# Three message-passing layers of a graph network: the order of TensorE's steps in the GATv2 loops, and of ScalarE's copies in the GAT loop

## The reference

```python
def _gatv2(x, src, dst, eattr, Wl, Wr, We, att, b, n):
    xl = x @ Wl
    xr = x @ Wr
    xj = xl[src]
    h = leaky_relu(xj + xr[dst] + eattr @ We, 0.2)
    logits = h @ att
    m = segment_max(logits, dst, n)
    ex = exp(logits - m[dst])
    denom = segment_sum(ex, dst, n)
    return segment_sum(xj * (ex / denom[dst])[:, None], dst, n) + b

# GAT, 4 heads of 64
h = (x @ W).reshape(-1, 4, 64)
e = leaky_relu(einsum('nhd,hd->nh', h, att_src)[src] + einsum('nhd,hd->nh', h, att_dst)[dst], 0.2)
m = segment_max(e, dst, n)
ex = exp(e - m[dst])
alpha = ex / segment_sum(ex, dst, n)[dst]
out = sigmoid(segment_sum(alpha[:, :, None] * h[src], dst, n) + bias)
```

## Time and profile before

| | |
|---|---|
| median of 3 runs | 6522.72 us (6521.69 to 6536.36) |
| the profiled execution's own time | 6535.35 us |
| its span in the profile | 6533.6 us |
| mean granted PE clock | 0.941 of full speed |
| busy share | PE 76%, DVE 71%, ACT 51%, POOL 48% |
| the three edge loops | 1474 + 1479 + 1518 = 4471 us |

### The profile page before, as it was taken

How to read it: one execution, slowest core, us unless ns; L and a number is a source line. 1 busy time by engine, 2 the same in 40 slices (tenths; PEclk the granted TensorE clock), 3 DMA queues, 4 the chain that set the end, 5 groups by cost and what they waited for, 6 DMA issues and landing times. The chain is left out here.

```text
span 6533.6 us, 112163 instructions
## 1 busy us (share of the span) xinstructions
PE 4991.3 (76%) x28188; PEld 3639.1 (56%) x28558; DVE 4608.6 (71%) x17132; ACT 3312.4 (51%) x8567; POOL 3155.9 (48%) x3442
## 2 busy tenths in 40 slices
PE   5999877985778777886687877777366766666799
PEld 2444444863656555664465655556255555555578
DVE  8999876254777777776577767777577777777721
ACT  5888765023555555553455545555355555555520
POOL 2444333634556555650565656554255555555400
PEclk9999988997999999998899999999689999999899
DMA  2233334853444444441444444443234443443264
GB/s 57 62 89 100 94 100 143 318 191 95 106 107 109 108 107 106 107 100 36 102 108 108 108 102 108 105 106 80 59 92 103 102 103 101 104 102 103 74 160 114
DMA packets 606739, 698.65 MB, mean 107 GB/s; under 512 B 243043, under 2 KB 512656, under 8 KB 599802
## 3 DMA queue, kind: packets, MB, share of 16 engines
q0 software_dynamic: 128832, 362.75, 22.0%
q1 hardware_dynamic: 477370, 329.75, 18.4%
HBM read 589.91 MB, written 102.19 MB: 106 GB/s over the span
## 5 line engine op out<-in xcount | busy, mean ns | idle before, releaser
L980 POOL DMA_INDIRECT gath<-table,src_col x880 | 846.7, 962 | 873.5 <-issue 601.8
L980 POOL DMA_INDIRECT h<-table,src_col x880 | 841.3, 956 | 574.9 <-issue 574.9
L1119 PE MATMUL psum<-xr 128*128 x3520 | 1031.8, 395 | 35.5 <-ACT xr L1081 18.0
L703 DVE SCALAR_TENSOR_TENSOR xr<-xr,gath,psum 128x259 f32<-128x259 f32 x1440 | 685.8, 476 | 108.0 <-PE psum L687 82.2
L1068 ACT CAST rows<-psum 128x128 bf16<-128x128 f32 x440 | 116.7, 265 | 1134.0 <-remote 684.8
L1204 POOL DMA_INDIRECT gath<-table,src_col x440 | 423.6, 963 | 490.3 <-issue 327.3
L1119 PEld LDWEIGHTS psum<-xr 128*128 128x128 f32 x3520 | 545.8, 196 | 200.5 <-issue 50.2
L999 DVE SCALAR_TENSOR_TENSOR zs<-zs,mean 128x256 f32<-128x256 f32 x1760 | 649.3, 423 | 0.0
L1005 DVE TENSOR_REDUCE seen<-psum 128x1 f32<-128x512 f32 x440 | 303.4, 690 | 470.5 <-PE psum L1130 321.4
L1204 POOL DMA_INDIRECT h<-table,src_col x440 | 422.0, 959 | 297.8 <-issue 297.8
L687 PE MATMUL psum<-zs,locrow 128*128 128x259 f32 x1440 | 468.1, 452 | 117.0 <-POOL zs L642 94.3
(11 more groups left out here) (330 smaller groups left out, 11988.3 us busy)
## 6 DMA issues: line engine op xcount, KB each, us to landing
locrow<-g_locb SPq DMA_DIRECT2D x660, 128.0 KB
pairs<-xr SPq DMA_DIRECT2D x640, 115.5 KB
xr<-pairs SPq DMA_DIRECT2D x13, 1716.0 KB
gath<-table,src_col POOLq DMA_INDIRECT x1320
h<-table,src_col POOLq DMA_INDIRECT x1320
xr<-pairs SPq DMA_DIRECT2D x25, 832.0 KB
acc<-pairs SPq DMA_DIRECT2D x12, 1716.0 KB
xr<-pairs SPq DMA_DIRECT2D x13, 1584.0 KB
```

Source lines behind the costliest of these rows:

```text
L703: nc.vector.scalar_tensor_tensor(kept[:, u, 0:EXTRA + 3], kept[:, (u - 1) % HELD, 0:EXTRA + 3], t["same"][:, g:g + 1], m.ps[u % 4][:, 0:EX ...
L980: pool.indirect_dma_start(m.gath[r][:, j, :], None, table, bass.IndirectOffsetOnAxis(m.src_col[r][:, j:j + 1], 0)).then_inc(gathered[r], 16)
L1119: nc.tensor.matmul(zb[q][:, j, :], m.hot[r][:, j, :], blk(m.xr, b, 0, D), start=True, stop=False)
```

## The change

In both GATv2 loops PE's list gives `turn_parts` a lag of 2 and a place ahead of `sum_group`; before, it stood at the head of the next step with lag 3. In the GAT loop the one-hots' copies go to three buffers in turn, the third a piece of `zs_all` that this loop doesn't use otherwise; `choose` waits for the group sum of three groups ago, `sum_group` reads the same buffer, and `choose` stands ahead of `copy_turned` on ACT.

```diff
--- before.py
+++ after.py
@@ -1140,7 +1140,7 @@
                                           start=(j == 0), stop=(j == T - 1))
                 mm.then_inc(group_sum, 1)
 
-            straight([(3, turn_parts), (4, flip), (3, show_logits), (1, mix), (4, sum_group)],
+            straight([(4, flip), (3, show_logits), (1, mix), (2, turn_parts), (4, sum_group)],
                       blocks_on(nc, m, mybir.EngineType.PE))
 
 
@@ -1170,6 +1170,7 @@
         here_ps = [m.ps[4 + q][:, K:2 * K] for q in (0, 1)]
         sum_ps = [m.ps[4 + q][:, 2 * K:2 * K + WA] for q in (0, 1)]
         rows = m.rows[:, :]
+        chosen_rows = [m.prob[:, 0, :], m.prob[:, 1, :], m.zs_all[:, 0:WIN]]
         room = m.xr3[:, :, :].rearrange("p b c -> p (b c)")
         ohT = [room[:, r * WIN:(r + 1) * WIN] for r in range(RG)]
         lgs = [room[:, RG * WIN + 2 * r * C:RG * WIN + 2 * (r + 1) * C].bitcast(F32) for r in range(RG)]
@@ -1368,15 +1369,15 @@
             def choose(t, u, turn, b):
 
                 act.wait_ge(flipped, t + 1)
-                after(act, group_sum, t, 2)
-                nc.scalar.copy(m.prob[:, u % 2, :], flip_ps[:, :]).then_inc(chosen, 1)
+                after(act, group_sum, t, 3)
+                nc.scalar.copy(chosen_rows[t % 3], flip_ps[:, :]).then_inc(chosen, 1)
 
             def shrinkage(t, u, turn, b):
                 r = u % R
                 act.wait_ge(dropped, t + 1)
                 nc.scalar.activation(m.less[r][:, 0:H], m.drop[:, 0:H], ACT.Exp).then_inc(shrink, 1)
 
-            straight([(4, copy_turned), (7, choose), (8, weigh), (6, shrinkage), (1, mask), (7, exponentials)])
+            straight([(7, choose), (4, copy_turned), (8, weigh), (6, shrinkage), (1, mask), (7, exponentials)])
 
         @block.tensor
         def _(pe):
@@ -1429,7 +1430,7 @@
                 pe.wait_ge(act_weighed, t + 1)
                 after(pe, done, t, 2)
                 for j in range(T):
-                    mm = nc.tensor.matmul(sum_ps[u % 2], m.prob[:, u % 2, j * P:(j + 1) * P], m.gath[u % RG][:, j, 0:WA],
+                    mm = nc.tensor.matmul(sum_ps[u % 2], chosen_rows[t % 3][:, j * P:(j + 1) * P], m.gath[u % RG][:, j, 0:WA],
                                           start=(j == 0), stop=(j == T - 1))
                 mm.then_inc(group_sum, 1)
```

## The result

The changed kernel took **6642.42 us** (median of 4 runs, 6617.16 to 6653.06) against 6522.2 us for the kernel before (6504.22 to 6536.36), a ratio of **1.0181** (95% interval 1.0152 to 1.0209). The profiled execution took 6617.16 us with a span of 6615.4 us, so it is the fastest of the four; the mean granted PE clock was 0.923, against 0.941.

The account below looks back on a forecast made before the run. It took POOL's trains of four gathers and the held release of PE's messages, 6.51 us a step, as the bound; 0 in GATv2 and -4.6 us in GAT gave 6518 us from the median 6522.72, range 6395 to 6625.

Parts of the forecast that it names:

- What bounds the kernel: Gather loops: PE's messages held during trains of four gathers, a period of 6.51 us set by POOL and the release.
- most steps must be like the one at 3256: GATv2 loops: most steps have a held message, as 6.45 and 6.54 us lie near the locked 6.51 us.
- Rival A: GATv2: messages late because of the order, not gathers; show_logits' 436 us of waits go, 6087 us; chance 0.08.
- The wait of show_logits: PE in GATv2 waits 263.1 and 172.8 us for ACT's copy of the turned parts; the change aims there.
- The price in GATv2: Group sum behind the turn waits for DVE's parts; sum and flips end 0.2 to 0.3 us later, 0.8 us to spare.
- Gain in a step in which the message is held: 0: GATv2: the earlier turn gains nothing, as the release hangs on the gathers and ACT's copy starts when it did.
- The term of 0 in the sum: The GATv2 loops' share of the forecast, 2 x 220 groups: no change in time, 0 us.
- The step without held messages: GATv2's new order with no message held: a chain of 5.10 us a step, under 6.51, so it does not bind.
- Rival C: GATv2: the turn's wait becomes the step, 6.96 us for 6.50 in half the steps, 6624 us; chance 0.17.
- in the locked step it comes in 0.03 us: GATv2: show's message reaches DVE in 0.03 us in a locked step, the reason for a chance of no more than 0.17.
- The gain of 4.6 us: GAT loop's end: seven steps without gathers each lose the flips' 0.65 us wait for choose; steps with gathers gain 0.

Follow-up runs that it names:

- e9: Kernel before with the GATv2 loops' gathers left out after the first ten groups, old order: 5920.3 us against 6548.61 us for the kernel before.
- e8: Kernel before with the GATv2 loops' loads of lin, locrow and eaT left out after the first five groups: 6512.92 us against 6548.61 us.
- e2: Kernel before with only the GAT part of the change: 5511.05 us against 5516.34 us, ratio 0.9991.
- e17: Kernel before with only the GAT part of the change, five rounds at the higher level: 6548.98 us against 6540.15 us, ratio 1.0006.
- e18: Kernel before with POOL's GATv2 gathers also waiting for DVE's parts of seven groups before: 6972.49 us against 6527.27 us, ratio 1.0685.
- e5: The whole change once more, against the kernel before at the lower level: 5559.02 us against 5520.4 us, ratio 1.0076.

## Why the prediction was wrong

*What bounds the kernel: right.* PE's messages are late in a train of gathers, and the gathers are the cause: 628 us by e9, against 36 for the loads in e8. One reading went too far: "most steps must be like the one at 3256". The turn ended there 4.24 us into a train of four, and so, within 4.2 to 4.4, it did in 199 of 440 steps; the mean of 6.50 us came from shorter and longer steps too.

The Trainium skill's rule that a DMA never contends with a compute engine ("SBUF — State Buffer", Who interferes with whom) doesn't tell what comes here. The trace agrees with it as to the engines' own work: the copy of the turned parts takes 0.27 us in a held step and in one that isn't. But the end messages of PE come late while gathers run at this level. Rival A, beside which it was named, gave 6087 us and did not come.

*The wait of show_logits: right as to where, wrong as to what follows.* It went (436 to 46 us), and what is late next was `parts`, as said.

*The price in GATv2, "0.2 to 0.3 us later ... with 0.8 us to spare", "Gain in a step in which the message is held: 0": this is the step that failed.* It took one step of the old rhythm, with the next release fixed at 3258.6 and with the messages of mix and show at once, as given, and moved PE's turn inside it. But the rhythm is a product of the order. The old one has the mix end 2.45 us into a train and come at once; the new one has sum, flips and show in a row behind a turn that waits, in many steps no pause that lets POOL's trains end after four, and trains of seven and eight, in one of which the mix is held for 3.9 us. The term of 0 in the sum was +103 us. The turn's wait was put at 0.1 us a step and was 474.6 us over 440 steps, 1.08 us; before, PE had waited 436 us, 0.99 us, in the other place. And the sum took PE's work as fixed, the group sum at 1.73 us: PE was busy for 146 us more, 119 of them in the group sum, while its waits fell by 43 us in all. How much of this is the clock behind the new pauses, and how much the longer trains, no run tells apart.

*The step without held messages, 5.10 us "under 6.51. So the new order alone does not bind": right in size, and of no use as a bound.* At the level of 5516 us it is 5.15 us against 5.06, and there it binds: 52 us. The estimate stood against 4.99 us for the old order in the rows without gathers, a difference of 0.11 us that could have been charged to every step in which nothing is held: 440 x 0.11 = 48 us.

*Rival C came, its number in part by luck.* 6624 us with a chance of 0.17, against 6642 measured. Its mechanism is there: `seen` out of "remote" for 374.2 us, where it was 134.6, and PE idle ahead of L1104. But it was to decide where the show's message is late in most steps, and `seen` came out of "remote" 104 times in 440; PE's longer busy time, 146 us, is not in it. It was held down by "in the locked step it comes in 0.03 us", again the old rhythm taken as fixed. The range ended at 6625 because C was priced for half of the steps; in all of them it would have been 6725, and 0.08 of it was left out.

*GAT: right in the total, not shown in the loop.* PE's wait at the flips (L1422, 383.3 us) is all but gone, and the waits of this loop are now

```profile
ACT ex L1350 <- issue: 452.2, 182, 3.9
...
PE psum L1401 <- DVE seen L1282: 194.7, 151, 2.2
```

so show_first, which waits for DVE's maximum, is late next, as said. The gain of 4.6 us agrees with -5.3 us (e2, interval -10.5 to +0.6 us) and isn't told apart from none. At the higher level the profiles have the loop shorter by some 20 us, more than the 4.6, and e17 as a whole no faster.

## What to carry to other kernels

A wait that is taken out of one place of a cycle through several engines turns up at the next instruction that waits for the same chain; so price a reorder by the chain from the new wait round to itself, at both rhythms that the trace shows, and not inside one old step. Then look at the engine's busy time as well as its waits: here the waits fell and the loop grew. An in-order engine on which everybody waits shouldn't have a long piece (here the group sum) put behind an instruction that waits for another engine's last result. And where a measurement can stand at two levels, compare only inside one series: the same edit cost 0.8% at one and 1.8% at the other.

## What was not expected of the hardware

The same kernel ran in 5516 us and in 6540 us, each steady over a series, on the same chip in different series, for two chips. At the higher level PE's end messages are held while POOL's indirect gathers run (1.56 us late in a train of four, 4.35 in one of seven, 5.4 in one of eight), by no other sign than the start of the waiting engine; and those that PE sends 2 to 4 us into a train of four come at once (e18). At the lower level the one in e5's step comes in 0.04 us with the same gathers at 5.04 us a group. What sets the level stayed open: nothing in these kernels chooses it.
